# A recurrence on one Trainium2 core: gate columns in four groups of 96

## The chip, the cores and the metric

The kernel runs on one core of a Trainium2 chip. The metric is the device time of one execution in microseconds (us); the time before is the median of three runs. One further execution was recorded by the hardware profiler; the trace's times come from it.

## The reference

The program is a small network: a GRU over the tokens, a differential attention, a filter and a full attention, and a mixture of experts. The change touches the GRU, which for four rows of 512 features takes 512 steps one after the other:

```python
def cell(h, x):
    gi = x @ W_ih + b_ih
    gh = h @ W_hh + b_hh
    i_r, i_z, i_n = jnp.split(gi, 3, axis=-1)
    h_r, h_z, h_n = jnp.split(gh, 3, axis=-1)
    r = jax.nn.sigmoid(i_r + h_r)
    z = jax.nn.sigmoid(i_z + h_z)
    n = jnp.tanh(i_n + r * h_n)
    h_new = (1.0 - z) * n + z * h
    return (h_new, h_new)
```

`W_ih` and `W_hh` are 512 x 1536, all in float32.

## The kernel before, in words

`gate_inputs_stage` (L55) comes first. TensorE transposes the four blocks of x, and VectorE spreads W_ih. SP's queue then loads W_hh into the tile `ahead` in 64 pieces (L104), after that 16 bias rows (L108). Then come the gate inputs: 17 row blocks of the products of x with W_ih (L163), which VectorE adds to the biases (L209) into three slots, and which SP stores to `gi_rows` in HBM (L113), each slot free again when its store has landed. After the third store SP loads the first 32 tokens of the rows back (L119). SP does all of this in program order.

`gru_stage` (L213) is the recurrence. The hidden state h stands transposed, as four chunks c of 128 features on the partitions, four batch rows each. A step's product with W_hh takes h as the stationary operand and W_hh's columns as the moving one: for each chunk c, four matmuls (j = 0 to 3) go to the four 32-column strips of the array, and write 32 rows each of PSUM. A float32 matmul is two weight loads and two matmul instructions in the trace. There are three sets of columns per strip: RZ (128 of r and the first 32 of z, 160 columns), N (128), and Z (the other 96 of z). The gate inputs of r and z, and the bias of n, are seeded into PSUM by ScalarE ahead of each step (L401, L405), into the half of PSUM that the step before does not use.

The step is written out by hand for each engine. TensorE (`step`, L353) waits for chunk 0 of h, multiplies RZ and N with it, waits for the other chunks, multiplies RZ, N and then Z with the rest. VectorE (`step`, L435) transposes the finished r rows (L437), the n rows in two parts (L441), scans n in two parts (L448, r times n plus its gate input), transposes z (L451), and with two scans writes h, chunk 0 first (L460). ScalarE (L396) does the sigmoid of r (L407), two tanh (L411) and the sigmoid of z (L413) between them. GpSimd copies the gate input of n (L325).

Ahead of each step TensorE runs a quarter of a product of the next 32 tokens with W_ih (`next_gate_input`, L368, L373): one matmul of 128 x 128. TensorE's loop body holds eight steps (L378), and runs 4 times inside an outer loop of 15 (L377); a last loop of 16 turns with two steps each follows (L383). VectorE and ScalarE have loops of their own, of four and of two steps.

Of the kernel before, what the change touches and what calls it, by code (L numbers as in the profile page):

```python
# [54 lines left out]
def gate_inputs_stage(nc, t, x, W_ih, b_ih, b_hh, h0, W_hh):  # L55
# [5 lines left out]
    with ExitStack() as ctx:  # L61
# [19 lines left out]
        NQ = 1 + NBL  # L81

        @block.sync
        def _(sp):
# [14 lines left out]
            whh = t.ahead[:].rearrange("p (c j g f) -> p c j g f", c=KD, g=3, j=KD)  # L99
            for jj in range(KD):  # L100
                rows = W_hh.rearrange("(jj c i) (g j f) -> jj i c j g f", jj=KD, c=KD, g=3, j=KD)[jj]
# [8 lines left out]
            for q in range(NQ):  # L110
                sp.wait_ge(row_out, q + 1)
                kb, gate = (0, 0) if q == 0 else (q - 1, 1)
                sp.dma_start(t.rows_dram[kb].rearrange("b t j f -> (b t) j f")[:, :, gate * P:(gate + 1) * P],  # L113
                             stage[:, q % NS, :].rearrange("p (j f) -> p j f", j=KD)).then_inc(stored[q % NS], 16)
                if q == 2:
                    sp.wait_ge(stored[0], 16)
                    sp.wait_ge(stored[1], 16)
                    for j in range(KD):
                        sp.dma_start(t.rows[32 * j:32 * j + B, 0:32, :], t.rows_dram[0][:, :, j, :]).then_inc(first_in, 16)  # L119
# [3 lines left out]
            sp.wait_ge(whh_in, 16 * KD * KD * KD)  # L123
            for n in range(NS):
                sp.wait_ge(stored[n], 16 * len(range(n, NQ, NS)))

# [53 lines left out]
        def _(dve):  # L180
# [24 lines left out]
            for q in range(NQ):  # L205
                dve.wait_ge(row_psum, q + 1)
                if q >= NS:
                    dve.wait_ge(stored[q % NS], 16 * (q // NS))
                nc.vector.tensor_tensor(stage[:, q % NS, :], pg[:, 2 + q % 2, :], t.gi_rbias[:] if q == 0 else rowb[:, 0, D:2 * D],  # L209
                                        ALU.add).then_inc(row_out, 1)  # L210


def gru_stage(nc, t, b_hh, next_weights):  # L213
# [8 lines left out]
    with ExitStack() as ctx:  # L222
# [6 lines left out]
        RZ, Z, N = slice(0, P + 32), slice(P + 32, 2 * P), slice(2 * P, 3 * P)  # L229
# [4 lines left out]
        tr = sb("tr", [P, KD + 1, 32])  # L234
        tn, tz, narg = sb("tn", [P, KD * 32]), sb("tz", [P, KD - 1, 32]), sb("narg", [P, ST, 2])
# [4 lines left out]
        prz = ctx.enter_context(nc.psum_tensor("gru_prz", [P, 2, 8 * P], F32))  # L240
        pn = ctx.enter_context(nc.psum_tensor("gru_pn", [P, 2, 4 * P], F32))
        pgi = ctx.enter_context(nc.psum_tensor("gru_pgi", [P, 4 * P], F32))
        R0, Z1, Z2 = 4 * P - (P + 32), 4 * P, 4 * P + P - 32
# [20 lines left out]
        def _(sp):  # L264
# [10 lines left out]
            def store_r(kb):  # L275
                sp.wait_ge(gi_out, kb * NG + KD + 1)
                sp.dma_start(t.rows_dram[kb + 1].rearrange("b t j f -> (b t) j f")[:, :, 0:P],
                             r_stage[:].rearrange("p (j f) -> p j f", j=KD)).then_inc(r_stored, 16)

            def load_rows(kb, js):  # L280
                sp.wait_ge(r_stored, 16 * (kb + 2))
                if kb > 0:
                    sp.wait_ge(rz_seeded, 32 * kb)
                for j in js:
                    sp.dma_start(t.rows[32 * j:32 * j + B, (kb + 1) % 2 * 32:(kb + 1) % 2 * 32 + 32, :],
                                 t.rows_dram[kb + 1][:, :, j, :]).then_inc(rows_in, 16)
# [50 lines left out]
        def _(pe):  # L337
            for n in range(2):
                for j in range(KD):
                    nc.tensor.matmul(pn[32 * j:32 * j + 32, n, 0:P], t.ident[:, 0:32], whh[:, 0, j, N], start=True, stop=True)  # L340
                    nc.tensor.matmul(prz[32 * j:32 * j + 32, n, R0:Z1], t.ident[:, 0:32], whh[:, 0, j, RZ], start=True, stop=True)
                    last = nc.tensor.matmul(prz[32 * j:32 * j + 32, n, Z1:Z2], t.ident[:, 0:32], whh[:, 0, j, Z], start=True, stop=True)
# [10 lines left out]
            def step(s, par):  # L353
                after = lambda c: t.h[:, 24 * B * c + 18:24 * B * (c + 1):24]
                places = lambda c: t.h[:, 24 * B * c:24 * B * (c + 1):3]
                rz_rows = lambda j: prz[32 * j:32 * j + B, par, R0:Z1]
                n_of = lambda j: pn[32 * j:32 * j + 32, par, 0:P]
                pe.wait_ge(h_ready[0], s * 1 + 1)
                pe.wait_ge(rz_seeded, s * 1 + 1)
                pe.wait_ge(n_seeded, s * 1 + 1)  # L360
                part(rz_rows, after, RZ, (0,))
                part(n_of, places, N, (0,))
                pe.wait_ge(h_ready[1], s * 1 + 1)
                part(rz_rows, after, RZ, (1, 2, 3), r_rows)
                part(n_of, places, N, (1, 2, 3), n_rows)
                part(lambda j: prz[32 * j:32 * j + B, par, Z1:Z2], after, Z, range(KD), z_rows)

            def next_gate_input(kb, c, k):  # L368
# [4 lines left out]
                last = nc.tensor.matmul(pgi[:, 0:P], left[:, k, :], right[:, k, :], start=(k == 0), stop=(k == KD - 1))  # L373
# [9 lines left out]
            with pe.Fori(T // 2 - 16, T // 2) as q:  # L383
                for par in range(2):
                    step(q * 2 + par, par)

        @block.scalar
        def _(act):
# [3 lines left out]
            nc.scalar.activation(prz[:, 0, R0:Z2], t.rows[:, 0, :], ACT.Copy).then_inc(rz_seeded, 1)  # L392
            nc.scalar.activation(pn[:, 0, 0:P], bias_rows[:], ACT.Copy).then_inc(n_seeded, 1)
            act.wait_ge(set_up, 4)

            def step(s, par):  # L396
# [4 lines left out]
                nc.scalar.activation(prz[:, 1 - par, R0:Z2], t.rows[:, bass.ds((s + 1) & 63, 1), :].rearrange("p o f -> p (o f)"),  # L401
                                     ACT.Copy).then_inc(rz_seeded, 1)
                act.wait_ge(tn_done[1], s * 1 + 1)
                act.wait_ge(tn_done[0], s * 1 + 1)
                nc.scalar.activation(pn[:, 1 - par, 0:P], bias_rows[:], ACT.Copy).then_inc(n_seeded, 1)  # L405
                act.wait_ge(tr_done, s * 1 + 1)
                nc.scalar.activation(cb(rd[:, 0:6 * (ST + B):6]), tr[:, :, 0:B], ACT.Sigmoid).then_inc(rz_act, 1)  # L407
                for n, part in enumerate(PARTS):
                    of = slice(part.start * B, part.stop * B)
                    act.wait_ge(narg_done[n], s * 1 + 1)  # L410
                    nc.scalar.activation(d0[:, of, 0:3:2], narg[:, of, 1:2].broadcast_to([P, of.stop - of.start, 2]), ACT.Tanh).then_inc(tanh_done[n], 1)  # L411
                act.wait_ge(tz_done, s * 1 + 1)
                nc.scalar.activation(cb(rd[:, 6 * (ST + B):12 * ST:6]), tz[:, :, 0:B], ACT.Sigmoid).then_inc(z_act, 1)  # L413
# [6 lines left out]
        def _(dve):  # L420
# [6 lines left out]
            dve.sem_inc(tn_done[0], 1)  # L427
            dve.sem_inc(tn_done[1], 1)
            dve.sem_inc(gi_out, 1)
            dve.sem_inc(r_stored, 16)  # L430
# [4 lines left out]
            def step(s, par):  # L435
                dve.wait_ge(r_rows, s * 1 + 1)
                nc.vector.transpose(tr[:].rearrange("p c x -> p (c x)"), prz[:, par, R0:Z1]).then_inc(tr_done, 1)  # L437
                dve.wait_ge(n_rows, s * 1 + 1)
                for n, part in enumerate(PARTS):
                    cols = slice(part.start * 32, part.stop * 32)  # L440
                    nc.vector.transpose(tn[:, cols], pn[:, par, cols]).then_inc(tn_done[n], 1)  # L441
                for n, part in enumerate(PARTS):
                    of = slice(part.start * B, part.stop * B)
                    dve.wait_ge(tn_done[n], s * 1 + 2)
                    if n == 0:
                        dve.wait_ge(rz_act, s * 1 + 1)
                        dve.wait_ge(gin_ready, s * 1 + 1)
                    nc.vector.tensor_tensor_scan(narg[:, of, :].rearrange("p c o -> p (c o)"), tn[:, part.start * 32 + 2:part.stop * 32:4],  # L448
                                                 rd[:, 6 * of.start:6 * of.stop:3], 0.0, ALU.mult, ALU.add).then_inc(narg_done[n], 1)
                dve.wait_ge(z_rows, s * 1 + 1)  # L450
                nc.vector.transpose(tz[:].rearrange("p c x -> p (c x)"), prz[:, par, Z1:Z2]).then_inc(tz_done, 1)  # L451
                for n, part in enumerate(PARTS):
# [6 lines left out]
                    of = slice(part.start * B, part.stop * B)  # L459
                    nc.vector.tensor_tensor_scan(t.h[:, 24 * of.start + 2:24 * of.stop + 2:8],  # L460
                                                 rd[:, ZB + 6 * of.start:ZB + 6 * of.stop:2], d0[:, of, :].rearrange("p c o -> p (c o)"),
                                                 0.0, ALU.mult, ALU.add).then_inc(h_ready[n], 1)
                dve.wait_ge(h_ready[1], s * 1 + 2)
# [3 lines left out]
            def keep_r(kb, c):  # L467
                dve.wait_ge(gi_psum, kb * NG + c + 1)
                dve.wait_ge(r_stored, kb * 16 + 16)
# [2069 lines left out]
```

## Time and profile before

| | us |
|---|---|
| median of three runs (lowest, highest) | 3850.36 (3848.35, 3858.16) |
| the profiled execution | 3852.93 |
| its span, first to last instruction | 3851.2 |
| TensorE busy in the span | 3555.0 (92%) |
| VectorE busy | 2109.0 (55%) |
| ScalarE busy | 1587.4 (41%) |
| granted TensorE clock, mean | 0.976 |

A busy TensorE is one with a matmul anywhere in its pipeline; it is not one at its peak. The steps of a recurrence can't overlap, so the order of events inside one step says more than the shares.

### The profile page before, as it was taken

To read this page: it belongs to the slowest core of one execution; us is meant where nothing else is said; L and a number is where in the kernel's file an instruction comes from. 1 tells how busy PE (TensorE), PEld (TensorE's weight loads), DVE (VectorE), ACT (ScalarE), POOL (GpSimd) and SP (SyncE) were. 2 spreads that over 40 slices of the span, in tenths; PEclk is the share of its full clock that TensorE was granted. 3 is DMA by queue.
4 is the path that set the end of the run, shared out by engine and by line. 5 is a ranking of instruction groups with operands and counts; after the bars stand their busy time and mean duration, and the time that the engine had idled before them with its cause. 6 is when DMAs were issued, how large, how long until landed. Compare 5 with 4: busy or idle time off the path is not lost. (4 is left out here: it accounts for less than half of the span.)

```text
span 3851.2 us, 151303 instructions
## 1 busy us (share of the span) xinstructions
PE 3555.0 (92%) x60904; PEld 2247.4 (58%) x60935; DVE 2109.0 (55%) x6359; ACT 1587.4 (41%) x4769; POOL 469.1 (12%) x973
## 2 busy tenths in 40 slices
PE   5899999999999999998799999968899999899999
PEld 2577878888888888886444444424433333455554
DVE  2355555555555555555477777744466666532228
ACT  0255555555555555554344444422344444321110
POOL 1000000000000000000122222200000000024430
PEclk8999999999999999999999999979999998999999
DMA  4222222211111111111111111020111111159987
GB/s 141 88 74 82 71 71 73 71 27 25 27 27 25 27 30 27 27 27 33 57 58 39 38 57 38 19 79 23 50 57 57 57 57 40 55 181 312 310 249 297
DMA packets 220456, 298.92 MB, mean 78 GB/s; under 512 B 19955, under 2 KB 159503, under 8 KB 216416
## 3 DMA queue, kind: packets, MB, share of 16 engines
q1 hardware_dynamic: 201536, 244.94, 20.5%
q10 hardware_dynamic: 8032, 25.70, 2.3%
q0 software_dynamic: 10816, 27.33, 2.2%
q8 instruction: 44, 0.72, 0.1%
q14 instruction: 28, 0.23, 0.0%
HBM read 156.83 MB, written 63.96 MB: 57 GB/s over the span
## 5 line engine op out<-in xcount | busy, mean ns | idle before, releaser
L348 PE MATMUL gru_prz<-ahead,h 128*4 128x160 f32 (+1 forms) x32768 | 1179.3, 273 | 37.9 <-DVE h L460 15.1
L348 PEld LDWEIGHTS gru_prz<-ahead,h 128*4 128x4 f32 x32768 | 722.4, 87 | 206.5 <-DVE h L460 111.7
L348 PE MATMUL gru_pn<-ahead,h 128*32 128x128 f32 x16384 | 636.1, 273 | 0.0
L348 PEld LDWEIGHTS gru_pn<-ahead,h 128*32 128x32 f32 x16384 | 509.4, 123 | 28.2
L437 DVE STREAM_TRANSPOSE gru_tr<-gru_prz 128x160 f32<-128x160 f32 x512 | 179.0, 350 | 392.5 <-PE gru_prz L348 392.5
L411 ACT ACTIVATE gru_d<-gru_narg 128x8 f32<-128x8 f32 (+1 forms) x1024 | 209.4, 216 | 258.8 <-DVE gru_narg L448 258.8
L325 POOL COPY gru_rd<-giT 128x16 f32 x512 | 110.2, 215 | 1556.9 <-DVE h L460 1556.9
L441 DVE STREAM_TRANSPOSE gru_tn<-gru_pn 128x32 f32<-128x32 f32 (+1 forms) x1024 | 195.2, 229 | 157.0 <-PE gru_pn L348 157.0
L977 DVE TENSOR_REDUCE da_mx<-da_ps 128x2 f32<-128x1024 f32 (+3 forms) x256 | 201.3, 817 | 131.9 <-PE da_ps L670 131.9
L407 ACT ACTIVATE gru_rd<-gru_tr 128x20 f32<-128x20 f32 x512 | 122.0, 238 | 350.5 <-DVE gru_tr L437 350.5
L373 PE MATMUL gru_pgi<-gru_right,gru_left 128*128 128x128 f32 x960 | 233.9, 325 | 25.4 <-issue 19.1
L460 DVE TENSOR_TENSOR_SCAN h<-gru_rd,gru_d 128x12 f32<-128x12 f32 (+1 forms) x1024 | 193.8, 189 | 114.8 <-ACT gru_rd L413 114.8
L884 ACT ACTIVATE da_probT<-da_ps 128x1024 f32<-128x1024 f32 (+3 forms) x256 | 169.4, 701 | 195.2 <-PE da_ps L691 192.5
L373 PEld LDWEIGHTS gru_pgi<-gru_right,gru_left 128*128 128x128 f32 x960 | 142.8, 188 | 113.9 <-issue 113.9
L401 ACT ACTIVATE gru_prz<-rows 128x256 f32 x512 | 198.6, 388 | 20.0
L601 POOL TENSOR_SCALAR_AFFINE_SELECT da_probT<-da_probT 128x256 f32<-128x256 f32 x256 | 141.7, 564 | 421.3 <-ACT da_probT L884 421.2
L399 ACT ACTIVATE gru_d<-h 128x16 f32<-128x16 f32 x512 | 123.4, 241 | 154.4 <-DVE h L460 154.4
L2149 PE MATMUL ex_pg<-ahead,ex_xT 128*128 128x384 f32 x512 | 175.8, 486 | 0.3 <-DVE ex_xT L2255 0.3
L1661 DVE TENSOR_REDUCE fa_mx<-fa_ps 128x2 f32<-128x1024 f32 x128 | 150.5, 1218 | 44.9 <-PE fa_ps L1480 44.8
L448 DVE TENSOR_TENSOR_SCAN gru_narg<-gru_tn,gru_rd 128x8 f32<-128x8 f32 (+1 forms) x1024 | 163.0, 170 | 0.0
L451 DVE STREAM_TRANSPOSE gru_tz<-gru_prz 128x96 f32<-128x96 f32 x512 | 144.9, 283 | 19.5 <-PE gru_prz L348 0.4
L1700 DVE TENSOR_TENSOR fa_total<-fa_total,fa_probT 128x2048 f32<-128x2048 f32 x48 | 109.9, 2290 | 55.1 <-ACT fa_probT L1601 55.1
(306 smaller groups left out, 4741.1 us busy)
## 6 DMA issues: line engine op xcount, KB each, us to landing
ahead<-in_L_ffn_gate_up_proj SPq DMA_DIRECT2D x64, 768.0 KB, 7.2
yk<-gru_zeros SPq DMA_DIRECT2D x29, 1024.0 KB, 5.0
ex_wd<-in_L_ffn_down_proj ACTq DMA_DIRECT2D x64, 384.0 KB, 6.6
ahead<-yk SPq DMA_DIRECT2D x16, 1536.0 KB, 9.1
gru_right<-ahead SPq DMA_DIRECT2D x60, 256.0 KB, 2.7
gru_left<-ahead SPq DMA_DIRECT2D x60, 256.0 KB, 2.7
ahead<-wide SPq DMA_DIRECT2D x15, 1024.0 KB, 4.7
ahead<-xnT SPq DMA_DIRECT2D x15, 1024.0 KB, 4.5
```

Of the source, the lines that this page charges most:

```text
L348: last = nc.tensor.matmul(rows(j), of(c), whh[:, c, j, cols], start=False, stop=True, skip_group_check=True)
L373: last = nc.tensor.matmul(pgi[:, 0:P], left[:, k, :], right[:, k, :], start=(k == 0), stop=(k == KD - 1))
L401: nc.scalar.activation(prz[:, 1 - par, R0:Z2], t.rows[:, bass.ds((s + 1) & 63, 1), :].rearrange("p o f -> p (o f)"), ACT.Copy).then_inc(rz ...
L411: nc.scalar.activation(d0[:, of, 0:3:2], narg[:, of, 1:2].broadcast_to([P, of.stop - of.start, 2]), ACT.Tanh).then_inc(tanh_done[n], 1)
L437: nc.vector.transpose(tr[:].rearrange("p c x -> p (c x)"), prz[:, par, R0:Z1]).then_inc(tr_done, 1)
L441: nc.vector.transpose(tn[:, cols], pn[:, par, cols]).then_inc(tn_done[n], 1)
L448: nc.vector.tensor_tensor_scan(narg[:, of, :].rearrange("p c o -> p (c o)"), tn[:, part.start * 32 + 2:part.stop * 32:4], rd[:, 6 * of.sta ...
L460: nc.vector.tensor_tensor_scan(t.h[:, 24 * of.start + 2:24 * of.stop + 2:8], rd[:, ZB + 6 * of.start:ZB + 6 * of.stop:2], d0[:, of, :].rea ...
L884: nc.scalar.activation(probT[:, n % 2, 2 * part:2 * part + 2, n * P:T], ps[:, KBANK[2 * part]:KBANK[2 * part] + 2, n * P:T], ACT.Exp, scal ...
L977: nc.vector.tensor_reduce(mx[:, i, a, 2 * part:2 * part + 2], ps[:, bank:bank + 2, 0:(i + 1) * P], AX, ALU.max).then_inc(max_done, 1)
L1661: nc.vector.tensor_reduce(mx[:, i, 2 * half:2 * half + 2], ps[:, 2 * half:2 * half + 2, :], AX, ALU.max).then_inc(max_done, 1)
L2149: last = nc.tensor.matmul(pg[:, u % 2, 0:2 * I], xT[:, u % 2, k, :], wg[:, u, k, :], start=(k == 0), stop=(k == KD - 1))
```

## The change

The three column sets become four of 96 columns for each strip: FIRST (32 of r, 32 of z and 32 of n, all of feature chunk 0), R1 (the other 96 of r), N1 (the other 96 of n) and Z (the other 96 of z). FIRST is transposed in one go, so that the sigmoid, the scan, the tanh and the new h of chunk 0 follow from it alone. All four sets use 32 stationary columns per strip, of which four carry h. Chunk 0 of h now meets all four sets before the wait for the other chunks. W_hh is stored in this column order: 96 load DMAs where 64 were, and each store of gate inputs becomes two. ScalarE's seed of r and z becomes two, and a wait for the transpose of FIRST stands ahead of Z on TensorE. The gate-input product is issued as four matmuls of 32 stationary columns. The main loop's body has eight steps as before; the last loop has 8 turns of four steps.

The core of the diff:

```diff
+        PIECES = ((0, 0, F0), (32, 1, F0), (64, 2, F0), (96, 0, F1), (192, 2, F1), (288, 1, F1))
+        ROWS = ((0, 1, F1), (96, 0, F0), (128, 1, F0), (160, 0, F1))
...
-                    for j in range(KD):
-                        sp.dma_start(whh[32 * jj:32 * jj + 32, c, j, :, :], rows[:, c, j, :, :]).then_inc(whh_in, 16)
+                    for to, g, f in PIECES:
+                        sp.dma_start(whh[32 * jj:32 * jj + 32, c, :, to:to + f.stop - f.start], rows[:, c, g, :, f]).then_inc(whh_in, 16)
...
-        RZ, Z, N = slice(0, P + 32), slice(P + 32, 2 * P), slice(2 * P, 3 * P)
+        FIRST, R1, N1, Z = slice(0, 96), slice(96, 192), slice(192, 288), slice(288, 3 * P)
...
             def step(s, par):            # TensorE
-                part(rz_rows, after, RZ, (0,))
-                part(n_of, places, N, (0,))
+                part(rows(first_of), places, FIRST, (0,))
+                part(rows(r1_of), places, R1, (0,))
+                part(rows(n1_of), places, N1, (0,))
+                part(rows(z_of), places, Z, (0,))
                 pe.wait_ge(h_ready[1], s * 1 + 1)
-                part(rz_rows, after, RZ, (1, 2, 3), r_rows)
-                part(n_of, places, N, (1, 2, 3), n_rows)
-                part(lambda j: prz[32 * j:32 * j + B, par, Z1:Z2], after, Z, range(KD), z_rows)
+                part(rows(first_of), places, FIRST, (1, 2, 3), first_rows)
+                part(rows(r1_of), places, R1, (1, 2, 3), r1_rows)
+                part(rows(n1_of), places, N1, (1, 2, 3), n1_rows)
+                pe.wait_ge(t0_done, s * 1 + 1)
+                part(rows(z_of), places, Z, (1, 2, 3), z_rows)
...
-                last = nc.tensor.matmul(pgi[:, 0:P], left[:, k, :], right[:, k, :], start=(k == 0), stop=(k == KD - 1))
+                for j in range(KD):
+                    last = nc.tensor.matmul(pgi[32 * j:32 * j + 32, 0:P], left[:, k, 32 * j:32 * j + 32], right[:, k, :],
+                                            start=(k == 0), stop=(k == KD - 1))
...
-            with pe.Fori(T // 2 - 16, T // 2) as q:
-                for par in range(2):
-                    step(q * 2 + par, par)
+            with pe.Fori(T // 4 - 8, T // 4) as q:
+                for k in range(4):
+                    step(q * 4 + k, k % 2)
...
+                nc.scalar.activation(zrz_of(1 - par), row[:, 0:160], ACT.Copy).then_inc(rz_seeded, 1)
+                nc.scalar.activation(r1_of(1 - par), row[:, 160:2 * P], ACT.Copy).then_inc(r1_seeded, 1)
...
+                dve.wait_ge(first_rows, s * 1 + 1)            # VectorE
+                turn(t0, first_of).then_inc(t0_done, 1)
+                dve.wait_ge(rz0_act, s * 1 + 1)
+                dve.wait_ge(gin_ready, s * 1 + 1)
+                dve.wait_ge(t0_done, s * 1 + 1)
+                scan_n(slice(0, B), t0[:, 2, 2:32:4]).then_inc(narg_done[0], 1)
+                dve.wait_ge(r1_rows, s * 1 + 1)
+                turn(tr1, r1_of).then_inc(tr1_done, 1)
+                scan_h(0)
+                dve.wait_ge(n1_rows, s * 1 + 1)
+                turn(tn1, n1_of).then_inc(tn1_done, 1)
+                dve.wait_ge(tn1_done, s * 1 + 2)
+                dve.wait_ge(r1_act, s * 1 + 1)
+                scan_n(slice(B, ST), tn1[:].rearrange("p c x -> p (c x)")[:, 2:96:4]).then_inc(narg_done[1], 1)
+                dve.wait_ge(z_rows, s * 1 + 1)
+                turn(tz, z_of).then_inc(tz_done, 1)
+                scan_h(1)
```

`turn` is a transpose of VectorE; `scan_n` and `scan_h` are the two scans that were there before. ScalarE's order in a step is now: copy of h, three seeds, sigmoid of r0 and z0, tanh of chunk 0, sigmoid of r1, tanh of the rest, sigmoid of z.

## Rows read from the trace of the kernel before

**Rows 1.** Windows, the recurrence: length, busy time of each engine, clock, DMA.

```profile
140.00:1848.00 1708.00, 1642.61 (x50145) 1356.89 (x50140) 927.62 (x4728) 869.84 (x3586) 128.25 (x542) 1.00 0.17 45
```

**Rows 2.** Timeline of TensorE, one step: start, length, instruction, count, idle before.

```profile
802.13 1.00 PE L348 MATMUL gru_prz<-ahead,h 128*4 128x160 f32 x24
802.94 0.84 PE L348 MATMUL gru_pn<-ahead,h 128*32 128x128 f32 x24
803.60 0.84 PE L348 MATMUL gru_prz<-ahead,h 128*4 128x96 f32 x32
...
805.40 0.46 PE L348 MATMUL gru_prz<-ahead,h 128*4 128x160 f32 x8
```

**Rows 3.** Timeline of VectorE, the same step.

```profile
803.85 0.38 DVE L441 STREAM_TRANSPOSE gru_tn<-gru_pn 128x32 f32<-128x32 f32 x2 [0.30 <-PE gru_pn L348]
804.15 0.32 DVE L448 TENSOR_TENSOR_SCAN gru_narg<-gru_tn,gru_rd 128x8 f32<-128x8 f32 x2
804.51 0.28 DVE L451 STREAM_TRANSPOSE gru_tz<-gru_prz 128x96 f32<-128x96 f32 x1
804.71 0.14 DVE L460 TENSOR_TENSOR_SCAN h<-gru_rd,gru_d 128x12 f32<-128x12 f32 x1
805.08 0.23 DVE L460 TENSOR_TENSOR_SCAN h<-gru_rd,gru_d 128x36 f32<-128x36 f32 x1 [0.23 <-ACT gru_rd L413]
```

**Rows 4.** Timeline of ScalarE, the same step.

```profile
802.07 0.24 ACT L399 ACTIVATE gru_d<-h 128x16 f32<-128x16 f32 x1 [0.30 <-DVE h L460]
802.35 0.39 ACT L401 ACTIVATE gru_prz<-rows 128x256 f32 x1
...
803.58 0.24 ACT L407 ACTIVATE gru_rd<-gru_tr 128x20 f32<-128x20 f32 x1 [0.64 <-DVE gru_tr L437]
...
804.82 0.23 ACT L413 ACTIVATE gru_rd<-gru_tz 128x12 f32<-128x12 f32 x1
```

**Rows 5.** Lines L348 and L460: count, ns min/median/max, first and last start.

```profile
L348 PEld LDWEIGHTS gru_prz<-ahead,h x32768: 84/87/131, 143.5 to 1845.5; 128*4 128x4 f32 x200
...
L348 PEld LDWEIGHTS gru_pn<-ahead,h x16384: 121/122/177, 143.7 to 1844.8; 128*32 128x32 f32 x200
...
L460 DVE TENSOR_TENSOR_SCAN h<-gru_rd,gru_d x1024: 140/190/241, 146.6 to 1846.5; 128x12 f32<-128x12 f32 x171
```

**Rows 6.** SP's timeline and the waits of the entry, 0 to 142 us.

```profile
26.54 42.07 SPq L104 DMA_DIRECT2D ahead<-in_L_cond_W_hh  x64
...
DVE gi_xin L209 <- DMA gi_rows<-gi_xin: 38.8, 2, 22.9
...
PE gi_pg L163 <- DVE gi_xin L209: 28.1, 2, 17.5
```

**Rows 7.** Instruction queues, 142 to 170 and 170 to 1735 us: packets, MB, share.

```profile
q8 instruction: 6, 0.10, 1.5%
...
q14 instruction: 3, 0.02, 0.0%
```

**Rows 8.** Groups by form, 300 to 1800 us: count, busy us, mean ns.

```profile
L451 DVE STREAM_TRANSPOSE gru_tz<-gru_prz 128x96 f32<-128x96 f32 x450 | 127.3, 283 | 17.2 <-PE gru_prz L348 0.4
...
L411 ACT ACTIVATE gru_d<-gru_narg 128x8 f32<-128x8 f32 x451 | 94.1, 209 | 228.1 <-DVE gru_narg L448 228.1
...
L448 DVE TENSOR_TENSOR_SCAN gru_narg<-gru_tn,gru_rd 128x8 f32<-128x8 f32 x451 | 59.8, 133 | 0.0
```

**Rows 9.** Timeline at the end of an eight-step body.

```profile
807.93 0.30 PEld L373 LDWEIGHTS gru_pgi<-gru_right,gru_left 128*128 128x128 f32 x2 [0.45 <-issue]
```

**Rows 10.** Timeline of TensorE behind the main loop's exit.

```profile
1744.46 0.44 PE L348 MATMUL gru_prz<-ahead,h 128*4 128x160 f32 x2 [3.37 <-issue]
```

**Rows 11.** Windows behind the exit; the granted clock is the third number from the end.

```profile
1744.00:1745.00 1.00, 0.54 (x12) 0.49 (x15) 0.00 (x0) 0.00 (x0) 0.00 (x0) 0.50 1.06 213
```

**Rows 12.** Timeline of VectorE there, h of two steps.

```profile
1739.78 0.23 DVE L460 TENSOR_TENSOR_SCAN h<-gru_rd,gru_d 128x36 f32<-128x36 f32 x1 [0.22 <-ACT gru_rd L413]
...
1748.12 0.24 DVE L460 TENSOR_TENSOR_SCAN h<-gru_rd,gru_d 128x36 f32<-128x36 f32 x1 [0.22 <-ACT gru_rd L413]
```

More of the change, by code:

```diff
@@ L98, in _ @@
             sp.wait_ge(w_spread, 3 * KD)
-            whh = t.ahead[:].rearrange("p (c j g f) -> p c j g f", c=KD, g=3, j=KD)
+            whh = t.ahead[:].rearrange("p (c j n) -> p c j n", c=KD, j=KD)
             for jj in range(KD):
-                rows = W_hh.rearrange("(jj c i) (g j f) -> jj i c j g f", jj=KD, c=KD, g=3, j=KD)[jj]
+                rows = W_hh.rearrange("(jj c i) (g j f) -> jj i c g j f", jj=KD, c=KD, g=3, j=KD)[jj]
                 for c in range(KD):
-                    for j in range(KD):
-                        sp.dma_start(whh[32 * jj:32 * jj + 32, c, j, :, :], rows[:, c, j, :, :]).then_inc(whh_in, 16)
+                    for to, g, f in PIECES:
+                        sp.dma_start(whh[32 * jj:32 * jj + 32, c, :, to:to + f.stop - f.start], rows[:, c, g, :, f]).then_inc(whh_in, 16)
             sp.wait_ge(zero_set, 2)
@@ L112, in _ @@
                 kb, gate = (0, 0) if q == 0 else (q - 1, 1)
-                sp.dma_start(t.rows_dram[kb].rearrange("b t j f -> (b t) j f")[:, :, gate * P:(gate + 1) * P],
-                             stage[:, q % NS, :].rearrange("p (j f) -> p j f", j=KD)).then_inc(stored[q % NS], 16)
+                for to, g, f in ROWS:
+                    if g == gate:
+                        sp.dma_start(t.rows_dram[kb].rearrange("b t j f -> (b t) j f")[:, :, to:to + f.stop - f.start],
+                                     stage[:, q % NS, :].rearrange("p (j f) -> p j f", j=KD)[:, :, f]).then_inc(stored[q % NS], 16)
                 if q == 2:
-                    sp.wait_ge(stored[0], 16)
-                    sp.wait_ge(stored[1], 16)
+                    sp.wait_ge(stored[0], 32)
+                    sp.wait_ge(stored[1], 32)
                     for j in range(KD):
-                        sp.dma_start(t.rows[32 * j:32 * j + B, 0:32, :], t.rows_dram[0][:, :, j, :]).then_inc(first_in, 16)
+                        sp.dma_start(t.rows[32 * j + 6:32 * j + 32:8, 0:32, :], t.rows_dram[0][:, :, j, :]).then_inc(first_in, 16)
             sp.wait_ge(first_in, 16 * KD)
@@ L122, in _ @@
             sp.wait_ge(hin_in, 16 * KD * KD)
-            sp.wait_ge(whh_in, 16 * KD * KD * KD)
+            sp.wait_ge(whh_in, 16 * KD * KD * len(PIECES))
             for n in range(NS):
-                sp.wait_ge(stored[n], 16 * len(range(n, NQ, NS)))
+                sp.wait_ge(stored[n], 32 * len(range(n, NQ, NS)))
         @block.gpsimd
@@ L339, in _ @@
                 for j in range(KD):
-                    nc.tensor.matmul(pn[32 * j:32 * j + 32, n, 0:P], t.ident[:, 0:32], whh[:, 0, j, N], start=True, stop=True)
-                    nc.tensor.matmul(prz[32 * j:32 * j + 32, n, R0:Z1], t.ident[:, 0:32], whh[:, 0, j, RZ], start=True, stop=True)
-                    last = nc.tensor.matmul(prz[32 * j:32 * j + 32, n, Z1:Z2], t.ident[:, 0:32], whh[:, 0, j, Z], start=True, stop=True)
+                    for k, cols in enumerate((slice(0, 96), slice(320, 512), slice(0, 96))):
+                        last = nc.tensor.matmul(ps[32 * j:32 * j + 32, n, k, cols], t.ident[:, 0:32], whh[:, 0, j, 0:cols.stop - cols.start],
+                                                start=True, stop=True)
             last.then_inc(opened, 1)
@@ L400, in step @@
                 act.wait_ge(rows_in, ((s + 1) >> 5) * (16 * KD) + 16 * KD)
[L401 to L411, printed above, removed]
+                row = t.rows[:, bass.ds((s + 1) & 63, 1), :].rearrange("p o f -> p (o f)")
@@ L435, in step, with scan_n, scan_h @@
             def step(s, par):
[L436 to L442, printed above, removed]
-                    of = slice(part.start * B, part.stop * B)
[L444 to L452, printed above, removed]
+                def scan_n(of, rows_of_n):
+                    return nc.vector.tensor_tensor_scan(narg[:, of, :].rearrange("p c o -> p (c o)"), rows_of_n,
+                                                        rd[:, 6 * of.start:6 * of.stop:3], 0.0, ALU.mult, ALU.add)
+                def scan_h(n):
+                    part = PARTS[n]
+                    of = slice(part.start * B, part.stop * B)
                     if n == 0:
@@ L462, in step, with turn @@
                                                  0.0, ALU.mult, ALU.add).then_inc(h_ready[n], 1)
+                def turn(to, of):
+                    return nc.vector.transpose(to[:].rearrange("p c x -> p (c x)"), of(par))
+                dve.wait_ge(first_rows, s * 1 + 1)
[15 more added lines that the diff above has]
+                scan_h(1)
                 dve.wait_ge(h_ready[1], s * 1 + 2)
```

64 lines of the change are left out of this document (38 added, 26 removed).

## The prediction

> **What bounds the kernel now.** I read the table of windows first: the recurrence is 1,708 of 3,851 us, TensorE at full clock and almost always counted busy [rows 1]. A busy row of matmuls proves nothing, so the next view is the order of events of one step on each engine. On TensorE [rows 2] the reader is to see four blocks: 24 matmul instructions of r and the first z columns, 24 of n, 32 of z, then a gate-input product, and at 805.40 the next step begins, 3.27 us after 802.13. On VectorE and ScalarE [rows 3, 4] the end of each instruction is followed within 0.03 to 0.04 us by the one it releases. Followed back from the end of the second scan into h (805.08 + 0.24 = 805.32), the chain is: sigmoid of z (804.82), transpose of z (804.51), the two scans of n (804.15), the transposes of n (803.85), and before those the n rows. So one step is 0.08 us from h to the first matmul, 1.72 us until the n rows are out (802.13 to 803.85), and 1.47 us of VectorE and ScalarE: 3.27 us. Over the stage the mean is (1846.5 - 146.6)/511 = 3.327 us [rows 5]; the 0.05 us above 3.28, about 25 us in all, belong to the loop ends, where TensorE's sequencer comes late.
>
> Two facts outside the step matter. First, at the entry 64 DMAs of W_hh take 42.07 us on SP's queue, and behind them stand the bias rows and then the stores of the gate inputs; VectorE waits for a store's landing once for 22.9 us, and TensorE behind it [rows 6]. Second, the instruction queue of TensorE fetched six packets, 0.10 MB, during the first pass through the loop body, and none from 170 to 1735 us [rows 7]: the body has stayed on the chip for 59 further passes.
>
> **The step, part by part.** Groups of four matmul instructions start every 0.81/6 = 0.135 us at 160 columns, 0.66/6 = 0.110 us at 128, and (0.84 - 0.25)/7 = 0.08 us at 96 [rows 2]; I use 0.082. Six groups (three chunks of h, two instructions each) are 0.49 us, and from the last group's start to the transpose there is 0.25 us more, as 803.85 - 802.94 - 0.66 shows [rows 2, 3]. So the first group's rows are out 0.74 us after the start, not 1.72 us.
>
> What follows has become longer: t0 is a 96-column transpose, 0.28 us, as that of z [rows 8]; then 0.04 us to ScalarE, sigmoid 0.22, 0.03 back, scan 0.13, 0.03, tanh 0.21, 0.03 [rows 8], and the scan of h0, after whose start the next instruction can begin 0.07 us later (804.71 stands 0.08 us before the end of the transpose ahead of it, and I take the same overlap here). Then the transpose of n1 0.28, 0.03, its scan 0.13 until the next may start, the transpose of z 0.28, 0.03, sigmoid 0.22, 0.03, scan 0.24. The sum is 2.28 us. The transpose of r1 and its sigmoid lie beside the tanh of the first group; should they not be hidden, VectorE pays 0.20 us more. The z rows are ready 24 x 0.082 + 0.25 = 2.22 us after the start, and VectorE reaches them at 0.74 + 1.48 = 2.22 us: a tie, so each nanosecond that a group loses costs 24.
>
> The new step is 0.08 + 0.74 + 2.28 = 3.10 us, 0.17 less than 3.27; over 512 steps **-87 us**. Bounds of the unknown overlaps: with 0.24 us for the n1 transpose and tighter hops -110, with the r1 transpose wholly on the path +15.
>
> The other edits of the step are covered. ScalarE's seeds become three: copy 0.24 from 0.03 us after h, then some 0.23, 0.17 and 0.26 us by their columns (256 take 0.39 [rows 4]), ending near 0.96, just ahead of the sigmoid at 1.06; without that cover each 0.1 us is 51 us. TensorE's chunk 0 has 8 groups, 0.66 us, where 288 columns took 0.50; it must fit between the end of z (1.97 us) with the product (0.22 to 0.3 us) and the next h (3.02): it ends at 2.93. The product in four narrow parts moves the same 128 columns per instruction; it lies where TensorE now waits for h, so I give it nothing. At the loop end it does show: there TensorE stands 0.45 us before the product [rows 9], so 1.97 + 0.45 + 0.25 + 0.66 = 3.33 us against 3.10, some 0.25 us late per eight steps, with a smaller lateness in mid-body, instead of today's 25 us in all: **+15 us** (0 to +30). The added wait for t0 before z is long met (0.74 + 0.28 against 1.48); behind it stand the z matmuls and the next product.
>
> **The entry.** W_hh goes in 96 pieces, not 64. At 42.07/64 = 0.66 us of SP's queue each that is 32 x 0.66 = +21 us, ahead of the bias rows and of every store, for which VectorE and TensorE already wait; nothing covers it. Each of the first three stores becomes two DMAs: three more at the same price, +2 us. Each later pair of stores has the matmuls of a whole row block to hide behind. Sum **+23 us** (+10 if issue gets cheaper with smaller pieces, +35 if dearer).
>
> So far -87 + 15 + 23 = -49 us: 3,852.9 - 49 = about 3,804 us. The profiled execution took 3,852.9 us, 1.7 us around its span and 2.5 above the median of the three runs.
>
> **The code.** This decides. Today a step has (32,768 + 16,384)/512 = 96 weight loads and as many matmul instructions [rows 2, 5]; with the product's four, eight steps are 1,568, plus some 25 for registers and branches. At 0.10 MB for 1,593 they have about 64 bytes each. The change has 16 matmuls per group instead of three groups of 16: 128 and 128 per step, the product 16; eight steps are 2,176, with the rest some 2,210: 0.14 MB, nine to ten packets. The loop body is still eight steps. No row shows a body above seven packets kept. If the first packets have been written over when the branch goes back, each of the 59 repeats waits for them.
>
> What a late packet costs, one place shows: after the loop's exit TensorE finds a packet late, stands 3.37 us, and runs on at half clock (0.50 from 1744 to 1745) [rows 10, 11]; the step takes 1748.12 - 1739.78 = 8.34 us instead of 3.27, +5.07 [rows 12]. There the DMA queues were full of weights, so this is the upper end; the lower is the bare idle time less what the branch waits already, 3.37 - 0.45 = 2.9 us. I take 4.4 us, nearer the row, since an idle TensorE falls to half clock there too: 59 x 4.4 = **+260 us** (171 to 299 for one stall in each pass). Total 3,804 + 260 = 4,064, rounded to **4,060 us**.
>
> The Trainium skill, page "Runtime: NRT & Kernel Launch", section "Instruction fetch mechanics", says that TensorE's instruction memory holds 2,048 instructions and that a taken branch to a block outside it forces a fetch before execution goes on. By that rule a body of 1,593 stays and one of 2,210 does not; rows 7 agree with the first half, and no row of this case shows the second.
>
> **The rivals.** *The code is kept, or fetched in time* (faster): then 3,804 us. For it: first-pass packets came without any stall. It decides if a body of 0.14 MB is kept where 0.10 MB was. Chance 0.20.
>
> *Two stalls in each pass*: the branch target lies near the end of its packet, so the next packet is needed at once, or each packet comes late in turn because eight steps now need nine of them in 25 us. 3,804 + 2 x 260 = about 4,320 us. Against it: the first pass. Chance 0.20.
>
> *Weight loads hold the matmuls*: all loads now have 32 columns, and one takes 122 ns instead of 87 [rows 5]. Four-column loads of 87 ns run unseen under groups of 82 ns, so a load's length alone does not bind; were the 35 ns to show in each of 24 groups, 0.84 us per step, it would be 430 us: about 4,230 without stalls of code. Chance 0.08. The page "TensorE: Matmul & The Clock Gate", section "LDWEIGHTS (loading the stationary operand)", puts a load at columns/1.2 ns; one after the other, four would be an estimated 107 ns per group, over the 82. No row separates that, since n runs at 110.
>
> *Nothing gained and nothing lost*: the tie at the z rows or the r1 transpose eats the step's gain and code is kept, 3,850 us, chance 0.05.
>
> **How the numbers follow.** The forecast's case has 0.47, with its own range 3,975 to 4,103. About 0.3% is what a measurement of this kernel can tell from no change. Faster takes the code-kept case, 0.20; same 0.05; slower 0.75. The range from 3,775 to 4,350 reaches over the kept code (less its best end) and the two stalls: left out are some 0.06 below and 0.13 above.
>
> **What would show it.** Right: instruction packets of TensorE's queue all through 170 to 1735 us, TensorE idle for over 2 us once in eight steps ended by "issue", half clock behind it, and between those stalls steps of about 3.10 us with the first transpose 0.74 us after the first matmul. W_hh's issue ends near 90 us and the recurrence begins near 164. Wrong: no packets there; groups of 96 columns starting further apart than 0.085 us; steps of 3.27 us or more in mid-body; an entry that ends at 138 us as now.

## The result and the profile after

The changed kernel takes 4,659.8 us (median of four runs, 4,639.9 to 4,665.4) where the kernel before took 3,851.4 beside it: a ratio of 1.209, 95% interval 1.205 to 1.213, 808 us slower. The forecast was 4,060 us, range 3,775 to 4,350.

The page of the changed kernel, its first, second, third and fifth parts (line, engine, operation, count | busy us, mean ns | idle us before, releaser):

```profile
span 4660.5 us, 191958 instructions
...
PE 3772.0 (81%) x80199; PEld 2535.5 (54%) x80199; DVE 2198.6 (47%) x6359; ACT 1738.1 (37%) x5794; POOL 469.9 (10%) x973
...
q8 instruction: 698, 11.44, 1.1%
...
L356 PE MATMUL gru_ps<-ahead,h 128*32 128x96 f32 x65536 | 1778.1, 260 | 304.3 <-issue 286.6
...
L385 PE MATMUL gru_pgi<-gru_right,gru_left 128*32 128x128 f32 x3840 | 256.5, 297 | 353.0 <-issue 338.8
```

L356 holds the four column groups, L385 the product in four parts. TensorE stands 286.6 + 338.8 = 625 us in front of these two for nothing that the profile shows but its own issue. The window of the recurrence, which was 1,708 us at full clock [rows 1]:

```profile
140.00:2653.00 2513.00, 1853.95 (x69256) 1643.45 (x69247) 1016.66 (x4725) 1018.85 (x4602) 128.51 (x540) 0.90 0.12 34
```

It is 805 us longer: the whole loss lies there. The DMA view of 500 to 1500 us, where none of TensorE's packets came before [rows 7]:

```profile
q8 instruction: 271, 4.44, 2.1%
```

That is one packet of instructions every 1000/271 = 3.7 us, without end. One pass through the loop body, VectorE's timeline, the second scan into h of each step:

```profile
1511.43 0.23 DVE L464 TENSOR_TENSOR_SCAN h<-gru_rd,gru_d 128x36 f32<-128x36 f32 x1 [0.29 <-ACT gru_rd L429]
1522.16 0.23 DVE L464 TENSOR_TENSOR_SCAN h<-gru_rd,gru_d 128x36 f32<-128x36 f32 x1 [0.29 <-ACT gru_rd L429]
1525.33 0.23 DVE L464 TENSOR_TENSOR_SCAN h<-gru_rd,gru_d 128x36 f32<-128x36 f32 x1 [0.29 <-ACT gru_rd L429]
1528.65 0.23 DVE L464 TENSOR_TENSOR_SCAN h<-gru_rd,gru_d 128x36 f32<-128x36 f32 x1 [0.29 <-ACT gru_rd L429]
1533.93 0.24 DVE L464 TENSOR_TENSOR_SCAN h<-gru_rd,gru_d 128x36 f32<-128x36 f32 x1 [0.29 <-ACT gru_rd L429]
1538.50 0.23 DVE L464 TENSOR_TENSOR_SCAN h<-gru_rd,gru_d 128x36 f32<-128x36 f32 x1 [0.29 <-ACT gru_rd L429]
...
1550.53 0.23 DVE L464 TENSOR_TENSOR_SCAN h<-gru_rd,gru_d 128x36 f32<-128x36 f32 x1 [0.29 <-ACT gru_rd L429]
```

The first step of the pass takes 10.73 us, the next two 3.17 and 3.32, and the other five 4.0 to 5.3: 39.1 us for eight. TensorE's timeline of the same pass shows why:

```profile
1515.97 0.65 PE L385 MATMUL gru_pgi<-gru_right,gru_left 128*32 128x128 f32 x8 [5.14 <-issue]
...
1518.51 2.88 PE L356 MATMUL gru_ps<-ahead,h 128*32 128x96 f32 x100 [0.79 <-issue]
...
1528.91 0.41 PE L385 MATMUL gru_pgi<-gru_right,gru_left 128*32 128x128 f32 x2 [0.83 <-issue]
...
1532.94 0.37 PE L356 MATMUL gru_ps<-ahead,h 128*32 128x96 f32 x4 [0.86 <-issue]
...
1537.32 0.47 PE L356 MATMUL gru_ps<-ahead,h 128*32 128x96 f32 x12 [0.81 <-issue]
1541.08 0.72 PE L356 MATMUL gru_ps<-ahead,h 128*32 128x96 f32 x24 [0.58 <-issue]
```

After the branch back it stands 5.14 us (4.5 to 6.7 over the 59 branches, median 5.1). Later it stands again, 0.6 to 0.9 us each time, before 1528.91, 1532.94, 1537.32 and 1541.08, some 4 us apart. Windows behind the branch (granted clock third from the end):

```profile
1515.90:1516.90 1.00, 0.93 (x24) 0.77 (x28) 0.00 (x0) 0.00 (x0) 0.00 (x0) 0.50 0.06 16
...
1518.90:1519.90 1.00, 1.00 (x32) 1.00 (x28) 0.00 (x0) 0.00 (x0) 0.00 (x0) 0.53 0.05 16
1519.90:1520.90 1.00, 1.00 (x59) 1.00 (x55) 0.56 (x3) 0.28 (x2) 0.00 (x0) 1.00 0.00 0
```

So the long stall is paid a second time: nearly 4 us at the 1.2 GHz level, until about 1519.9. The short ones are not: the granted clock is 1.00 from 1523 to 1550 us.

The step itself is seen in the last loop, where TensorE stands for no packet and runs no gate-input product (VectorE's timeline):

```profile
2560.69 0.28 DVE L469 STREAM_TRANSPOSE gru_t<-gru_ps 128x96 f32<-128x96 f32 x1 [0.53 <-PE gru_ps L356]
2561.26 0.17 DVE L452 TENSOR_TENSOR_SCAN gru_narg<-gru_t,gru_rd 128x8 f32<-128x8 f32 x1 [0.29 <-ACT gru_rd L421]
...
2561.71 0.18 DVE L464 TENSOR_TENSOR_SCAN h<-gru_rd,gru_d 128x12 f32<-128x12 f32 x1
2561.81 0.26 DVE L469 STREAM_TRANSPOSE gru_tn<-gru_ps 128x96 f32<-128x96 f32 x1
2562.11 0.21 DVE L452 TENSOR_TENSOR_SCAN gru_narg<-gru_tn,gru_rd 128x24 f32<-128x24 f32 x1
2562.23 0.26 DVE L469 STREAM_TRANSPOSE gru_tz<-gru_ps 128x96 f32<-128x96 f32 x1
2562.79 0.23 DVE L464 TENSOR_TENSOR_SCAN h<-gru_rd,gru_d 128x36 f32<-128x36 f32 x1 [0.30 <-ACT gru_rd L429]
...
2563.86 0.28 DVE L469 STREAM_TRANSPOSE gru_t<-gru_ps 128x96 f32<-128x96 f32 x1 [0.52 <-PE gru_ps L356]
```

From t0 to t0 it is 3.17 us (forecast 3.10; before 3.27 in [rows 2], 3.28 in the median). TensorE's row there, 256 instructions in 6.11 us for two steps, holds no stall but the wait for h.

The entry, SP's queue, and below it VectorE's wait for stores:

```profile
26.54 48.51 SPq L107 DMA_DIRECT2D ahead<-in_L_cond_W_hh  x96
75.09 4.73 SPq L111 DMA_DIRECT2D bias_rows<-in_L_cond_b_hh  x16
79.86 4.07 SPq L118 DMA_DIRECT2D gi_rows<-gi_xin  x6
```

```profile
DVE gi_xin L214 <- DMA gi_rows<-gi_xin: 33.6, 3, 30.3
```

W_hh's issue takes 6.4 us more, not 21, and the waits for stores are 33.6 us in sum where they were 38.8 [rows 6]: the recurrence begins some 6 us earlier, not 23 later.

### The profile page after: what moved, and what is told of

Its sections match the earlier page's. It is cut to its first block and busy times, and to the rows that moved or that the text cites. A ratio compares the mean times of both kernels' runs of the same rounds, so it can differ in the third digit from the quotient of the medians.

```text
span 4660.5 us, 191958 instructions
## 1 busy us (share of the span) xinstructions
PE 3772.0 (81%) x80199; PEld 2535.5 (54%) x80199; DVE 2198.6 (47%) x6359; ACT 1738.1 (37%) x5794; POOL 469.9 (10%) x973
## 5 line engine op out<-in xcount | busy, mean ns | idle before, releaser
L356 PE MATMUL gru_ps<-ahead,h 128*32 128x96 f32 x65536 | 1778.1, 260 | 304.3 <-issue 286.6
L356 PEld LDWEIGHTS gru_ps<-ahead,h 128*32 128x32 f32 x65536 | 1584.9, 129 | 475.6 <-issue 391.4
L385 PE MATMUL gru_pgi<-gru_right,gru_left 128*32 128x128 f32 x3840 | 256.5, 297 | 353.0 <-issue 338.8
L469 DVE STREAM_TRANSPOSE gru_t<-gru_ps 128x96 f32<-128x96 f32 x512 | 145.0, 283 | 734.5 <-PE gru_ps L356 733.7
L385 PEld LDWEIGHTS gru_pgi<-gru_right,gru_left 128*32 128x32 f32 x3840 | 129.2, 116 | 392.7 <-issue 392.7
L469 DVE STREAM_TRANSPOSE gru_tz<-gru_ps 128x96 f32<-128x96 f32 x512 | 141.7, 277 | 187.8 <-PE gru_ps L356 187.5
L429 ACT ACTIVATE gru_rd<-gru_tz 128x12 f32<-128x12 f32 x512 | 116.2, 227 | 204.5 <-DVE gru_tz L469 200.5
L469 DVE STREAM_TRANSPOSE gru_tn<-gru_ps 128x96 f32<-128x96 f32 x512 | 138.8, 271 | 110.6 <-PE gru_ps L356 110.2
L416 ACT ACTIVATE gru_ps<-rows 128x160 f32 x512 | 157.7, 308 | 19.6
L469 DVE STREAM_TRANSPOSE gru_tr<-gru_ps 128x96 f32<-128x96 f32 x512 | 139.4, 272 | 15.6 <-PE gru_ps L356 15.4
```

What stands on the lines that cost most here:

```text
L356: last = nc.tensor.matmul(rows(j), of(c), whh[:, c, j, cols], start=False, stop=True, skip_group_check=True)
L385: last = nc.tensor.matmul(pgi[32 * j:32 * j + 32, 0:P], left[:, k, 32 * j:32 * j + 32], right[:, k, :], start=(k == 0), stop=(k == KD - 1))
L416: nc.scalar.activation(zrz_of(1 - par), row[:, 0:160], ACT.Copy).then_inc(rz_seeded, 1)
L469: return nc.vector.transpose(to[:].rearrange("p c x -> p (c x)"), of(par))
```

## The experiments

Theory A: a body of 2,210 instructions is fetched anew in each pass, and packets of some 256 instructions come at a fixed pace, which the new step outruns. Rival B: each packet has a stall of its own, whatever its instructions take. Rival C: the size of the body doesn't matter, and the new step is slow. Body sizes are worked out as in the prediction, not read from a trace.

**e1: four steps per pass.** The product's index runs on, so one loop does for all.

```diff
-            with pe.Fori(0, NBL - 1) as kb:
-                with pe.Fori(0, NG // 2) as c2:
-                    for cc in range(2):
+            with pe.Fori(0, (NBL - 1) * NG) as p:
                         for k in range(KD):
-                            next_gate_input(kb, c2 * 2 + cc, k)
-                            step(kb * 32 + c2 * (2 * KD) + (cc * KD + k), k % 2)
+                            next_gate_input(p, k)
+                            step(p * KD + k, k % 2)
```

> The changed kernel, TensorE's main loop with four steps per pass instead of eight (about 1,105 instructions instead of 2,210), everything else as changed. Theory A (the body of eight steps is fetched anew in each of 60 passes, one packet of some 256 instructions about every 4 us): no instruction packets inside the recurrence, steps of 3.17 us, recurrence some 1,650 to 1,675 us, total 3,790 to 3,815. Rival C (the new step itself is slow: the three seeds, the four narrow parts, the 32-column loads): total stays near 4,600.

3,795.9 us, ratio 0.984 (0.982 to 0.986): 864 us less than with eight steps, and faster than the kernel before. TensorE's waits from 500 to 1500 us (sum, times, longest), first with eight steps:

```profile
PE gru_pgi L385 <- issue: 147.3, 53, 6.7
PE gru_ps L356 <- issue: 117.4, 154, 1.4
```

and with four:

```profile
PE gru_ps L356 <- DVE h L463: 2.4, 10, 0.2
PE gru_pgi L385 <- issue: 0.5, 3, 0.2
```

No instruction packet of TensorE comes in that stretch. Rival C falls: the step is the same, and only TensorE's loop is another. That it is one loop now and not two nested ones is not the reason: e11 has the same single loop with sixteen steps, and its packets come all through. The scans into h run from 137.8 to 1788.7 us, 1,650.9 us, against 1,699.9 before [rows 5].

**e2 and e3: the kernel before, with twelve and with forty steps per pass**, by the same edit with three and ten products in the body.

> The kernel before, nothing changed but TensorE's main loop: twelve steps per pass (about 2,390 instructions, 40 passes) instead of eight (1,593, 60 passes). Theory A (packets come at a fixed pace of about 4 us; a packet is 256 instructions, which the old step uses up in 4.2 us, so only the branch back waits, some 5 us): 40 x 5 = +200, total 4,030 to 4,080. Rival B (every packet costs a stall of its own of about 0.7 us, however long its instructions last): 40 x 9.3 x 0.7 = +260 more, total near 4,310. Rival C (the size of the loop body doesn't matter): 3,850.

> The kernel before with forty steps per pass (about 7,900 instructions, 12 passes). Theory A: 12 x 5 = +60, less the ends of 48 passes at about 0.4 us: total 3,880 to 3,915. Rival B: 12 x 31 x 0.7 = +260 and the 60: total near 4,150. Rival C: below 3,850.

e2 takes 4,105.7 us, ratio 1.064 (1.062 to 1.066). Its h at a branch back, on VectorE:

```profile
1023.68 0.23 DVE L459 TENSOR_TENSOR_SCAN h<-gru_rd,gru_d 128x36 f32<-128x36 f32 x1 [0.22 <-ACT gru_rd L412]
1033.42 0.23 DVE L459 TENSOR_TENSOR_SCAN h<-gru_rd,gru_d 128x36 f32<-128x36 f32 x1 [0.22 <-ACT gru_rd L412]
1036.70 0.23 DVE L459 TENSOR_TENSOR_SCAN h<-gru_rd,gru_d 128x36 f32<-128x36 f32 x1 [0.22 <-ACT gru_rd L412]
```

One step in twelve takes 9.74 us, 6.5 more than the others, which stay at 3.28: 40 x 6.5 = 260 us, less some 17 that the ends of the eight-step body take in the kernel before, against 247 measured (4,105.7 - 3,858.9, the kernel before beside it). The packets are fetched (243 in 1,000 us), but between branches none is late, since the old step uses one up in 256/199 x 3.28 = 4.2 us. That is A with a dearer branch (it had 5 us, and so 4,080 at most), and not B. e3, a single run, takes 4,002 us, between both. Its eleven branches back and the exit take 78 us more than bare steps. Most of the rest is another wait, which neither theory had:

```profile
L373 PE MATMUL gru_pgi<-gru_right,gru_left 128*128 128x128 f32 x960 | 238.0, 330 | 117.2 <-issue 44.7 <-DMA gru_left<-ahead 35.2 <-DMA gru_right<-ahead 33.8
```

69 us of waiting for the weights of the gate-input products, 2.4 us in the kernel before. 3,859 + 78 + 69, less the 17, is 3,989 of 4,002. Why those weights land late in the second half of a long pass stays open.

**e4, e8, e10: shorter bodies of eight steps.** All have the product as one matmul again; e8 and e10 also leave work out of the step.

```diff
-                for j in range(KD):
-                    last = nc.tensor.matmul(pgi[32 * j:32 * j + 32, 0:P], left[:, k, 32 * j:32 * j + 32], right[:, k, :],
-                                            start=(k == 0), stop=(k == KD - 1))
+                last = nc.tensor.matmul(pgi[:, 0:P], left[:, k, :], right[:, k, :], start=(k == 0), stop=(k == KD - 1))
```

> The changed kernel with the gate-input product as one matmul of 128 stationary columns again, eight steps per pass: about 2,105 instructions instead of 2,210. Theory A with a limit at 2,048 instructions: all packets are still fetched in each pass, 0.4 packet less, 4 us x 0.4 x 60 = -100, total near 4,560. If the limit lies above 2,105 instructions: no packets in the recurrence, total near 3,800. Rival C (the narrow parts are what is slow): well below 4,400 with packets or without.

> The changed kernel with eight steps per pass, the gate-input product as one matmul, and three of the four strips of z's last chunk left out of the computation in every step: some 2,017 instructions per pass instead of 2,209. Theory A with a limit of 2,048 instructions: no packets in the recurrence, steps of 3.17 us, total near 3,795. Rival L (the limit lies lower, or the body must fit whole packets): packets all through, 9.7 x 3.7 us = 36 us per pass, total near 4,400.

> The changed kernel with eight steps per pass and the product as one matmul, chunk 3 of h left out of the n and z products of columns N1 and Z in every step: some 1,857 instructions per pass. If a body is kept up to eight packets less the two that are fetched beyond its end (some 1,540 to 1,800): packets all through, 9 x 3.65 us = 33 us per pass, total near 4,230. If it is kept up to some 1,900 or more: no packets, total near 3,810.

4,455, 4,406 and 4,322 us, a single run each: packets all through in each, 273, 275 and 261 in 1,000 us. The pace stays the same, 3.6 to 3.8 us, and fewer packets per pass are all that is won. e4 came out 105 us faster than theory A said, since a pass has a whole packet less, 10.0 and not 11.0; e10 came out 92 us slower, at 3.8 us a packet and not 3.65. None of these bodies is kept, not even 1,857 instructions.

**e9: one part of the change alone**, the product in four narrow parts, put into the kernel before.

> The kernel before with one part of the change alone: the gate-input product as four matmuls of 32 stationary columns. The body of eight steps grows from 1,593 to 1,689 instructions. Theory (the narrow parts free TensorE some 0.2 us sooner, which counts only where TensorE is late for h, here at the loop end: 60 x 0.15): 5 to 12 us faster, ratio 0.997 to 0.999, no packets in the recurrence. Rival N (worth in every step what it was worth in the changed kernel, 30 us): 3,822. Rival L (1,689 instructions are already too many to be kept): near 4,100.

4,270.6 us, ratio 1.107 (1.106 to 1.109), from 96 more instructions in a pass: rival L, at a price 170 us higher than forecast, and the largest surprise of the study. Waits of TensorE from 500 to 1500 us, and its packets there:

```profile
PE gru_pgi L374 <- issue: 138.9, 29, 7.3
...
PE gru_prz L348 <- issue: 5.9, 20, 0.6
```

```profile
q8 instruction: 267, 4.37, 2.0%
```

The kernel before has 1,593 instructions and fetched none: it stood less than 100 below the limit. Whether the limit counts instructions, or the packets over which a body happens to lie, no run separates. Nearly all that is lost lies at the branch, as in e2: a step behind it takes 7.2 us more than 3.28 in the mean, the seven others of a pass 0.2 more together. The step uses 1,689/8 = 211 instructions, a packet in 4.0 us.

**e11: the changed kernel with sixteen steps per pass.**

> The changed kernel as it is, but sixteen steps per pass (about 4,400 instructions, 30 passes). Theory A (a pass takes its packets times 3.65 us: 17.2 of its own and the two beyond its end): 70 us per pass instead of 2 x 40.15, so 30 x 10.3 = 310 less, total near 4,350. Rival P (the branch back has a price of its own on top of the pace): the 30 branches that are gone take 30 x 8.6 = 260 with them, total near 4,400. Rival C: as with eight steps, 4,660.

4,422.6 us, a single run: 237 less than with eight, 7.9 us for each of the 30 branches that are gone. That is nearer to P than to A, and less than either; whether the branch has a price on top of the pace, this run does not settle. What a pass loses, and where, is read from the times between the scans into h. With eight steps the step behind a branch takes 8.6 us more than 3.17 in the mean of 59 passes, and the seven others, where packets come late in turn, 6.2 us more together. With sixteen it is 7.6 us behind a branch and 14.0 in the fifteen others.

**e5: four steps per pass, and the product as one matmul** (the edits of e1 and e4).

> The changed kernel with four steps per pass, and the gate-input product as one matmul of 128 stationary columns again instead of four of 32. Theory (the narrow parts lie where TensorE waits for h and are worth nothing): within 10 us of the four-step kernel with narrow parts, 3,786 to 3,806, ratio 0.981 to 0.987. Rival N (the narrow parts shorten the way to the next step's first matmuls): slower by more than 12 us, above 3,808.

3,825.9 us, ratio 0.993 (0.991 to 0.994), against 0.984 with narrow parts: rival N. TensorE's timeline with narrow parts, then with one matmul:

```profile
1005.49 0.40 PE L385 MATMUL gru_pgi<-gru_right,gru_left 128*32 128x128 f32 x8
1005.71 3.14 PE L356 MATMUL gru_ps<-ahead,h 128*32 128x96 f32 x128
```

```profile
1005.13 0.49 PE L384 MATMUL gru_pgi<-gru_right,gru_left 128*128 128x128 f32 x2
1005.54 2.87 PE L356 MATMUL gru_ps<-ahead,h 128*32 128x96 f32 x128
...
1008.76 2.87 PE L356 MATMUL gru_ps<-ahead,h 128*32 128x96 f32 x128
```

The next step's matmuls start 0.22 us after the narrow product and 0.41 after the wide one, and with the wide one TensorE no longer waits for h: the step is 3.22 us, 1005.54 to 1008.76. With narrow parts its weight loads wait for h in step after step (500 to 1500 us; sum, times, longest), a wait that e5 does not have:

```profile
PEld gru_ps L356 <- DVE h L463: 70.9, 234, 0.5
```

From the first h to the last, e5 takes 29 us more than e1, the same as the difference of the times.

**e6: the kernel before with the first rows loaded to spread partitions.**

```diff
-                        sp.dma_start(t.rows[32 * j:32 * j + B, 0:32, :], ...)
+                        sp.dma_start(t.rows[32 * j + 6:32 * j + 32:8, 0:32, :], ...)
```

> The kernel before; only the first load of 32 tokens of gate-input rows writes to partitions 6, 14, 22, 30 of each group of 32 instead of 0 to 3, so the first 32 tokens' gate inputs of r and z are left out of the computation. Theory D (in the kernel before this load to four neighbouring partitions is slow and holds three stores behind it for 17 to 20 us, and VectorE waits 15.94 us for them): that wait goes, the recurrence begins some 16 us earlier, total near 3,836. Rival S (it was the splitting of the stores that removed the wait): no change, 3,851.

3,836.9 us, ratio 0.996 (0.994 to 0.997): theory D. In the kernel before, the three stores issued behind these loads (80 to 85 us; KB each, us to landing):

```profile
gi_rows<-gi_xin SPq DMA_DIRECT2D x3, 256.0 KB, 19.7
```

In e6 the three stores issued from 78 to 86 us take 7.4 us (first line below), VectorE's waits for stores fall from 38.8 us [rows 6] to 28.7, and the first h stands at 132.4 us, 14 earlier than in [rows 5]. Why loads to neighbouring partitions are slow no run shows.

```profile
gi_rows<-gi_xin SPq DMA_DIRECT2D x3, 256.0 KB, 7.4
...
DVE gi_xin L209 <- DMA gi_rows<-gi_xin: 28.7, 2, 24.1
```

**e7: four steps per pass, and half of W_hh's pieces on ScalarE's queue**, the bias rows behind the stores.

```diff
-                for c in range(KD):
+                for c in (0, 2):
                     for to, g, f in PIECES:
                         sp.dma_start(whh[32 * jj:32 * jj + 32, c, :, to:to + f.stop - f.start], rows[:, c, g, :, f]).then_inc(whh_in, 16)
...
+            act.wait_ge(w_spread, 3 * KD)
+                for c in (1, 3):
+                    for to, g, f in PIECES:
+                        act.dma_start(whh[32 * jj:32 * jj + 32, c, :, to:to + f.stop - f.start], rows[:, c, g, :, f]).then_inc(whh_in, 16)
```

> The changed kernel with four steps per pass, and the entry rearranged: half of the 96 pieces of W_hh issued by ScalarE's queue instead of SP's, and the 16 bias rows behind the stores. Theory E (what delays the entry is SP's 48.5 us of issue ahead of the first store, not the transfers): the first store goes at about 51 us instead of 80, VectorE's wait of 30 us shrinks to below 8, total 3,770 to 3,778. Rival T (the transfers themselves are the limit, or ScalarE's issue holds the entry in its turn): 3,790 to 3,800.

3,773.3 us, ratio 0.979 (0.978 to 0.980): theory E, and the fastest of all; the two edits of the entry were not run apart. SP's queue, and VectorE's longest wait for a store that is left:

```profile
26.54 23.62 SPq L107 DMA_DIRECT2D ahead<-in_L_cond_W_hh  x48
50.27 5.11 SPq L114 DMA_DIRECT2D gi_rows<-gi_xin  x6
```

```profile
68.72 0.69 DVE L221 TENSOR_TENSOR gi_xin<-gi_pg,gi_rowb 128x512 f32<-128x512 f32 x1 [5.03 <-DMA gi_rows<-gi_xin]
```

## Why the prediction failed

The direction was right, and so was its cause, code fetched anew in every pass; **the term of the code failed**, +260 us predicted for one stall of 4.4 us in each pass. It is +864 us, 14.4 in each pass (e1), for two reasons. The step behind a branch takes 8.6 us more than a bare one (6.5 in e2, 7.2 in e9), where I had taken the price from the loop's exit [rows 10 to 12]: there TensorE stood 3.37 us in the middle of a step, with chunk 0 done and no product to run. At the branch it stands 5.1 us (median; 3.6 to 4.4 in e11, e2 and e9), and the product and all of chunk 0 still lie behind the stall, at half clock. And the packets come late in turn, another 6.2 us. (The two make 14.8; e1's own steps take some 0.5 in eight over 3.17, which is the difference.) The prediction had this as a rival, chance 0.20 and 4,320 us, and held "the first pass" against it. That argument was the error: the first pass of the kernel before showed only that packets come in time for a step that uses one in 4.2 us. The new one needs 276 instructions in 3.17 us, a packet in 2.9; the fetch gives one in 3.6 to 3.8 (e4, e8, e11 and the changed kernel alike). A row that shows no wait gives a bound on the supply, and I read it as the supply.

**Whether code is kept** was judged rightly, with 0.67 on the two cases of fetching. But the limit lies just above the kernel before: some 1,593 instructions are kept, 1,689 not (e9), so that the narrow parts alone would have done half of the damage, 416 of 808 us. The Trainium skill, page "Runtime: NRT & Kernel Launch", section "Instruction fetch mechanics", gives TensorE's instruction memory 2,048 instructions. By that figure the bodies of e8, e9 and e10 would have stayed; the runs show packets in all three, and the measurement decides. The section words its rule on a taken branch for the "current 2-page window", which the prediction read as the whole memory; as two blocks of 256 instructions it would have the 1,593 fetched too, and [rows 7] show that they are not.

**The step**, forecast 3.10 us, is 3.17; its parts agree within 0.05 us, and what is missing lies mostly in the first group, where scan to scan takes 0.45 us instead of 0.40 (the scan itself 0.17, not 0.13). Over 512 steps that is -56 us instead of -87.

**The loop end**, +15, is about +5: in e1, with twice as many loop ends, a step takes 1,650.9/511 = 3.23 us, 0.06 over the bare step, before 3.33 against 3.28. The forecast did not add up: 60 x 0.25 = 15 us stands against today's 25, and the lateness in mid-body that was to make up the rest had no number. There is none; the steps in mid-body take 3.18 us in e1. **The narrow parts**, costed at nothing, are worth 30 us with four steps (e5). I had TensorE waiting for h at that place. My own sum left only 0.09 us there (chunk 0 ending at 2.93, h at 3.02), and a wide product is 0.19 us longer.

**The entry**, +23, is some -6. W_hh's pieces cost 48.51/96 = 0.51 us, not 0.66, some +8 us with the three more stores, just below the lower bound named. What I didn't see is that the change also loads the first gate-input rows to partitions 6, 14, 22 and 30 of each 32, not 0 to 3; that takes away the wait of 15.9 us (the rest of the 38.8 in [rows 6]), and e6 shows that edit alone, 16 us.

**32-column weight loads** do not hold the matmuls: the bare step of 3.17 us has no room for 0.84. The estimate of 107 ns for four of them is not borne out either: in e5 128 go by in 2.66 us, 83 ns for four. The rivals "code is kept" and "nothing gained" fall with 271 packets in 1,000 us.

Together for the four-step kernel: step -56, loop end +5, entry -6 gives -57, 3,796 from 3,853; measured 3,795.9 (63 less than the kernel before beside it, which took 3,858.9). The forecast without code, 3,804, is near that by luck: the step gained 31 us less than forecast, and loop end and entry cost 39 less. The +864 of the eight steps is the difference of two measured times and no check of the sum.

## What to carry to other kernels

Count a loop body's instructions on its engine before you add any: here 96 more in some 1,593 cost 416 us, and halving the body turned a loss of 21% into a gain of 1.6%. Where code must be fetched, compare the pace of its packets with the time in which the work uses one up, and take the pace from a place where the engine waits for it. The stalls of 4 to 5 us at the branch were paid twice, once idle and once at the 1.2 GHz level behind them; those of 0.6 to 0.9 us were not.

## What the runs showed of the hardware

- TensorE's code came at nearly one pace: 261 to 275 packets in 1,000 us, 3.6 to 3.8 us each, in six kernels of 1,689 to some 4,400 instructions per pass. It was 243 in e2 and 227 in e3, where the step uses fewer.
- A body of some 1,593 instructions was kept over 59 passes, one of 1,689 fetched in each.
- In each pass about two packets more came than the body fills: 11.0 for 2,210 instructions (8.6 packets), 9.0 for 1,689 (6.6).
- A branch back to code that was not kept cost 6.5 to 8.6 us (e2, e9, e11 and the changed kernel).
- Loads of 4 x 128 KB to four neighbouring partitions in each 32 held the stores behind them for 19.7 us; spread over the 32 they held them for 7.4 (e6).
- 96 loads were issued in 48.5 us, 64 larger ones in 42.1 [rows 6].
